# A two-layer Mamba + mixture-of-experts kernel: layer 0's shared output added to X from PSUM, rows for the scatter kept in memory, four gathers ahead, 23 tiles, ScalarE's side pieces three steps later

## The reference, cut to what matters

```python
x = x + L0_xattn(ctx, layernorm(x), ...)   # conv, silu, delta, B, C, a scan over 512 positions with 16 states, * silu(z)
x = x + L0_ffn(layernorm(x), ...)          # below
x = x + L1_xattn(ctx, layernorm(x), ...)
x = x + L1_ffn(layernorm(x), ...)          # 8 experts, 2 for each row, shared expert of 1408 with a sigmoid gate

def L0_ffn(x):                             # 8 experts, 1 for each row
    logits = x @ router_w
    expert_idx, score = argmax(logits), sigmoid(max(logits))
    xs = x * score
    out[e rows] = (silu(xs @ gate_w[e]) * (xs @ up_w[e])) @ down_w[e]
    shared = (silu(x @ shared_gate_w) * (x @ shared_up_w)) @ shared_down_w
    return out + shared
```

## Time and profile before

| | |
|---|---|
| median of 3 runs | 2397.37 us |
| the profiled execution's own time | 2404.08 us |
| its span, first to last instruction | 2402.1 us |
| mean granted TensorE clock | 0.903 |
| busy: PE, DVE, ACT, POOL | 1959.0, 1415.0, 855.9, 989.3 us |
| SP's DMA queue | 326.21 MB, 39.7% of 16 engines |
| GpSimd's DMA queue | 25.17 MB, 3.1% |

### The profile page before, as it was taken

The page is one execution under the profiler, slowest core; times in us unless marked ns, Lnnn a source line. Parts: engine busy times, 40 slices in busy tenths (PEclk is TensorE's granted clock), DMA queues, the critical chain, the costliest instruction groups (busy, mean ns, idle before and its releaser), DMA issues. The chain is left out here.

```text
span 2402.1 us, 18775 instructions
## 1 busy us (share of the span) xinstructions
PE 1959.0 (82%) x5107; PEld 901.3 (38%) x5107; DVE 1415.0 (59%) x1962; ACT 855.9 (36%) x1392; POOL 989.3 (41%) x889
## 2 busy tenths in 40 slices
PE   8837678788787795599999973889599999999990
PEld 2212233233233341144444432445255555555540
DVE  6869988888887878797888844654010111111113
ACT  5545545364544444555656420110011111111110
POOL 0057766666575665887777731211400000000005
PEclk9968889899898997799999985999799999999995
DMA  5044354302203004368687645211654555455536
GB/s 185 22 194 105 140 110 107 112 5 99 89 8 153 1 14 155 138 225 339 224 305 277 215 153 189 68 50 58 242 179 152 180 180 166 160 179 180 175 123 214
DMA packets 100992, 352.50 MB, mean 147 GB/s; under 512 B 15200, under 2 KB 15200, under 8 KB 82464
## 3 DMA queue, kind: packets, MB, share of 16 engines
q1 hardware_dynamic: 93216, 326.21, 39.7%
q0 software_dynamic: 7680, 25.17, 3.1%
HBM read 288.29 MB, written 63.05 MB: 146 GB/s over the span
## 5 line engine op out<-in xcount | busy, mean ns | idle before, releaser
L561 POOL TENSOR_TENSOR work<-work,big 128x512 f32<-128x512 f32 x512 | 658.5, 1291 | 265.7 <-DVE bank L608 263.9
L474 PE MATMUL bank<-work,ident 128*128 128x512 f32 x928 | 536.9, 693 | 226.5 <-DVE work L592 175.9
L608 DVE TENSOR_TENSOR_SCAN bank<-bank,work 128x512 f32<-128x512 f32 x512 | 624.9, 1221 | 137.5 <-ACT bank L528 88.9
L528 ACT ACTIVATE bank<-work,An 128x512 f32<-128x512 f32 x512 | 345.9, 691 | 256.2 <-DVE work L592 253.1
L474 PEld LDWEIGHTS bank<-work,ident 128*128 128x128 f32 x928 | 179.5, 216 | 521.6 <-DVE work L592 333.7
L592 DVE TENSOR_TENSOR work<-bank,big 128x512 f32<-128x512 f32 x512 | 343.9, 672 | 9.1 <-PE bank L474 8.8
L1655 POOL DMA_INDIRECT W<-ys_d,slot x32 | 33.9, 1059 | 644.4 <-PEq L1642 634.9
L1612 PE MATMUL bank<-Y,big 128*128 128x512 f32 x528 | 263.6, 596 | 0.0
L1195 DVE SCALAR_TENSOR_TENSOR work<-work,bank 128x352 f32<-128x352 f32 (+1 forms) x63 | 36.6, 581 | 329.0 <-ACT work L1185 328.9
L957 PE MATMUL bank<-W,work 128*128 128x512 f32 x384 | 198.6, 622 | 0.0
L1173 ACT COPY work<-bank 128x512 f32<-128x512 f32 x63 | 36.9, 585 | 396.9 <-PE bank L1158 396.9
(11 more groups left out here) (249 smaller groups left out, 2252.8 us busy)
## 6 DMA issues: line engine op xcount, KB each, us to landing
big<-bc_d SPq DMA_DIRECT2D x64, 1024.0 KB, 6.7
work<-gate SPq DMA_DIRECT2D x39, 704.0 KB, 4.2
work<-up SPq DMA_DIRECT2D x39, 704.0 KB, 4.1
W<-gate SPq DMA_DIRECT2D x24, 1024.0 KB, 4.9
W<-up SPq DMA_DIRECT2D x24, 1024.0 KB, 5.5
W<-down SPq DMA_DIRECT2D x24, 1024.0 KB, 5.4
work<-down SPq DMA_DIRECT2D x39, 512.0 KB, 3.8
work<-xs_d SPq DMA_DIRECT2D x63, 256.0 KB, 4.4
```

Of the source, the lines that this page charges most:

```text
L474: nc.tensor.matmul(YS[:, :], ident[:, :], hC[ring(g * NS + u[0])], start=v == 0, stop=v == len(units[g]) - 1).then_inc(sum_done, 1)
L528: nc.scalar.activation(H[i % 4][:, :], delta[g % 2], ACT.Exp, scale=An[vb // B][:, g % NJ, i:i + 1]).then_inc(dA_done, 1)
L561: nc.gpsimd.tensor_tensor(dBu[i % 2], du[g % 2], Bb[:, i, :], ALU.mult).then_inc(dBu_done, 1)
L608: nc.vector.tensor_tensor_scan(H[i % 4][:, :], H[i % 4][:, :], dBu[i % 2], 0.0, ALU.mult, ALU.add).then_inc(scan_done, 1)
```

## The change

1. Layer 0's shared output stays in PSUM until VectorE adds it to X (`added`, 16 times, at the places where ScalarE copied it, the last of a batch in the very piece that makes it). `copy_y`, `yo`, `sh_d`, its 16 stores, its 16 loads and the 16 additions L1468 go.
2. X now no longer gives the normalised rows. So SP stores each `xn` to `xn_d` as it is made (16 stores, `xn_out`), SP loads them for the scatter, and ScalarE scales them by the router's weight. VectorE's `norm` and the gate's tanh of ScalarE, which overwrite `xn`, wait for these stores too.
3. In the scan ScalarE does its side pieces LAG = 3 steps after their place (`gate` excepted).
4. Layer 0 has 23 tiles of sorted rows and not 24.
5. Layer 1's feed-forward: four gather buffers and gathers issued four ahead; weights loaded in three widths, gate and up beside each other.
6. Small operations go: a copy of the mean on GpSimd, two on VectorE in the routing.

```diff
-        self.tiles += (self.tiles % 2, 0)[k]
...
-                    side.step("act", act, vb, n)
+                    if vb <= B:
+                        side.gate("act", act, vb, *divmod(n, NS))
+                    if s >= side.LAG:
+                        side.step("act", act, *divmod(s - side.LAG, NJ * NS))
+                for s in range(GROUPS * NS - side.LAG, GROUPS * NS):
+                    side.step("act", act, *divmod(s, NJ * NS))
...
             def gate(self, name, eng, b, j, i):
...
-                        self.past(eng, "xtr_done", b * NJ - NJ + (j + 1 if j else 0))
+                        used = b * NJ - NJ + (j + 1 if j else 0)
+                        self.past(eng, "xtr_done", used)
+                        self.past(eng, "xn_out", used * 16)
                     nc.scalar.activation(self.zth, v, ACT.Tanh).then_inc(self.S["zt_done"], 1)
...
+                    done = {(2, 3): 0, (3, 3): 1, (NJ, 1): NJ - 2, (NJ, 7): NJ - 1}.get((r, m))
+                    if done is not None:
+                        past(dve, "d_done", t0 + done + 1)
+                        nc.vector.tensor_tensor(X[:, t0 + done, :], X[:, t0 + done, :], self.TB[:, :], ALU.add).then_inc(S["added"], 1)
...
             def norm(self, dve, b, t0, r):
                 self.past(dve, "rstd_done", t0 + r + 1)
                 self.past(dve, "xtr_done", t0 + r)
+                self.past(dve, "xn_out", (t0 + r) * 16)
...
-                        act.wait_ge(S["y_out"], (t0 + max(r - 1, 0)) * 16 + 1)
                         nc.scalar.activation(self.sg, self.G[:, :], ACT.Tanh, scale=0.5).then_inc(S["s_done"], 1)
...
             def sync(self, sp, b, t0, n, at):
-                for r, m in at:
-                    for tile in ([r - 2] if m == 5 and 2 <= r else []) + ([NJ - 1] if r == NJ and m == 7 else []):
-                        self.past(sp, "yo_done", t0 + tile + 1)
-                        sp.dma_start(sh_d[t0 + tile], self.yo).then_inc(self.S["y_out"], 16)
+                for tile in ([0] if n == self.START - 1 else []) + [r + 1 for r, m in at if m == 6 and r < NJ - 1]:
+                    self.past(sp, "xn_done", t0 + tile + 1)
+                    sp.dma_start(xn_d[t0 + tile], self.xn).then_inc(self.S["xn_out"], 16)
...
             def scatter(self, name, eng, t):
-                if name == "act" and 0 <= t < T:
+                if name == "sp" and 0 <= t < T:
...
+                    eng.dma_start(self.rows[t % 8], xn_d[t]).then_inc(self.row_in[t % 8], 16)
+                if name == "act" and 0 <= t - 1 < T:
+                    t -= 1
...
+                    eng.wait_ge(self.row_in[t % 8], t // 8 * 16 + 16)
+                    nc.scalar.activation(self.rows[t % 8], self.rows[t % 8], ACT.Copy,
+                                         scale=wgt[:, 0, t:t + 1]).then_inc(self.row_done, 1)
...
+            WIDE = ((0, 2), (2, 6), (6, NF))
...
-                    for t in range(NJ):
-                        load(t)
...
+                    for c, (lo, hi) in enumerate(WIDE):
+                        for o in (0, FS):
+                            sp.dma_start(sgu[:, :, o + lo * P:o + hi * P], src[:, :, o + lo * P:o + hi * P]).then_inc(w_in[c], 16)
...
                     def gather(t):
-                        at_least(pool, C["x_done"], t - 1)
+                        at_least(pool, C["x_done"], t - 3)
...
-                            if p == r:
-                                dve.wait_ge(sh_in[t % 2], (t // 2 + 1) * 16)
-                                V.tensor_tensor(X_t, X_t, sh_b[t % 2], ALU.add).then_inc(C["sum_done"], 1)
```

More of the change, by code:

```diff
@@ L177, in program @@
         bc_d = dram("bc_d", [2 * B, 32, L])
-        sh_d = dram("sh_d", [T, P, D])
         xn_d = dram("xn_d", [T, P, D])
@@ L853, in step @@
                 last = isinstance(b, int) and b == B
-                if not last or n < NS:
+                if name != "act":
                     self.gate(name, eng, b, *divmod(n, NS))
@@ L863, in gate @@
             def gate(self, name, eng, b, j, i):
-                first = isinstance(b, int) and b == 0
-                if first and j == 0:
+                first = b == 0
+                if first and j == 0 or b == B and j:
                     return
@@ L1027, in scalar @@
                 for r, m in at:
-                    if m == 3 and 2 <= r < NJ:
-                        copy_y(r - 2)
                     if (m == 5 if r < NJ else m == 2) and r:
@@ L1218, in __init__ @@
                 self.row_done, self.out_done = sem("t0_row_done"), [sem(f"t0_scattered{q}") for q in range(8)]
+                self.row_in = [sem(f"t0_row_in{q}") for q in range(8)]
                 self.routed, self.cleared = sem("t0_routed"), sem("t0_rows_cleared")
@@ L1276, in step @@
                         eng.wait_ge(self.routed, 1)
-                        self.past(eng, "y_out", 16 * T)
+                        self.past(eng, "added", T)
+                        self.past(eng, "xn_out", 16 * T)
                     self.ex.before(name, eng)
@@ L1318, in stage_ffn1 @@
             v, zth = [wk(8 + j) for j in range(NJ)], [wk(12 + j) for j in range(NJ)]
-            sh_b, ys_b = [wk(16), wk(17)], [wk(18), wk(19)]
+            ys_b = [wk(16 + q) for q in range(4)]
             rows = [wk(14 + i) for i in range(6)]
@@ L1362, in _ @@
                 def _(sp):
-                    def load(t):
-                        at_least(sp, C["sum_done"], t - 1)
-                        sp.dma_start(sh_b[t % 2], sh_d[t]).then_inc(sh_in[t % 2], 16)
                     def keep(t):
```

80 lines of the change are left out of this document (29 added, 51 removed).

## The result

The kernel after takes **2450.41 us** (median of 4 runs, 2447.88 to 2454.62) beside 2398.09 of the kernel before (4 runs): ratio 1.0222, 95% interval 1.0200 to 1.0243. It is slower by 52 us; the forecast was 2383, range 2350 to 2410.

The account below looks back on a forecast made before the run. In scan batches 1 to 3 VectorE and TensorE stop each other; TensorE bounds batch 6 and the stretch from 1712 us. Terms summing to -14.2 took the profiled 2404.1 to 2389.9, or 2383.2 from the median; range 2350 to 2410.

Parts of the forecast that it names:

- store behind zeros(1), with the clock: Batch 1: tile 1's xn store lands behind the 9984 KB zeros on SP's queue; +51 us, plus 1.5 for TensorE's clock.
- no sh_d, batches 1 to 3: Scan batches 1 to 3: shared output added from PSUM ends waits for ScalarE's tanh and dA; -7 us each, -21.
- batch 4: Scan batch 4, frames packed in 36 steps, dA stalls following TensorE's lateness; -3 us, ends -8 and +3.
- scatter, batch 5: Batch 5: rows scaled by ScalarE after dA slow GpSimd's alternation of scatter and dBu; +5 us, ends 0 and +12.
- 23 tiles: End of scan: TensorE loses 16 passes and the last down product with its weight load; -17 us, ends 12 and 19.
- start and fronts of the feed-forward: Layer 1's feed-forward: -15.7 us at its start without the sh_d wait, -12 in the fronts of the other batches.
- ScalarE's pieces later: Batches 5 to 7: the later pieces remove part of VectorE's 40.9 us of waits for dA; -3 us, ends 0 and -9.
- Rival B: Scan: ScalarE's lateness costs what it saves, 1.4 us in each of 23 expert tiles; 2410 us, 18 in 100.
- Rival C: Scan: VectorE's waits for dA go wholly, half of 102.5 us of waits for ScalarE recovered; 2358 us, 15 in 100.
- term of -15.7: Start of layer 1's feed-forward: the 19.24 us sh_d wait goes, the fourth gather is late next; ends -11 and -20.
- The later fronts: Feed-forward's other three batches: each front loses four additions and 1 to 2 us of waits; -12 us, ends -8 and -14.4.
- The sign named for B: Scan: L1195 or TensorE waiting for ScalarE in every tile, and batches 6 and 7 over 155 us.

Follow-up runs that it names:

- LAG 0: Changed kernel with ScalarE's side pieces at their own step: 2373.91 us; with both zero stores also moved to step 10 of batch 0: 2320.79 us.
- zeros early: Changed kernel with both 9984 KB zero stores issued at step 10 of batch 0, ahead of any xn store: 2398.81 us.
- LAG 3 then 0: Changed kernel with both zero stores at step 10 of batch 0, ScalarE's side pieces three steps late only up to batch 4: 2367.02 us.
- LAG 1: Changed kernel with both zero stores at step 10 of batch 0 and ScalarE's side pieces one step late: 2313.14 us.

## Why the prediction was wrong, by its own steps

| step | forecast | measured | by |
|---|---|---|---|
| store behind zeros(1), with the clock | +52.5 | +51.6 (LAG 3), +53.1 (LAG 0) | zeros early |
| no sh_d, batches 1 to 3 | -21 | -20.2 | 486.5 to 466.3, 23 tiles alone against LAG 0 |
| batch 4 | -3 | -8.1 | 174.4 to 166.3, the same two |
| scatter, batch 5 | +5 | +2.0 | 162.8 to 164.8, the same two |
| 23 tiles | -17 | -17.3 | alone |
| start and fronts of the feed-forward | -27.7 | -34.3 | 923.5 to 889.2, the same two |
| **ScalarE's pieces later** | **-3** | **+76.5** | LAG 0 against LAG 3 |

All rows but the first and the last are read at LAG 0. The other terms were forecast at -11 in sum and came to -26 (the pause in it, +52.5 for 51.6 to 53.1), so they hid some 15 us of the miss of 79.5 in the last row; by the medians 67 was left. One step failed, *ScalarE's pieces later*: -3 us, with ends of 0 and -9, so with no end above nothing. It was costed by what it could take away (the 40.9 us for dA) and not by what it makes late. It does take those waits away, 40.9 to 2.5 us, and puts larger ones in their place.

Rival B had the mechanism and nearly its size, 1.4 us in each expert tile for 1.27 measured. It failed in its condition and in its price. The condition was that VectorE has 2.3 us to spare a tile in batch 6, from (151.9 - 130.8) / 9.1. That spare time is a mean; it lies in waits of other steps (for dA and dBu), and a wait put in front of the scan moves what comes after it. Added up for batches 5 to 7, VectorE's waits were 74.6 us before and 111.6 after, 37 us more; the three batches grew by 35.6. The price of B left out two things: the preparation of delta, which stands in the same list of ScalarE and turns 1.3 us into 4 to 8 in eight tiles (47 us of the 63.7), and batches 1 to 4, which pay 46 us by the run with LAG 3 then 0. Of these B had the larger part in words alone, that TensorE waits for the later copies; it gave it no price. The shared tiles' tanh had 1.4 us once a batch, in the term of batches 1 to 3; two tiles a batch wait for it, 2.1 and 4.9 us. Rival C's condition came true, the waits for dA went, and brought nothing, as the new waits were larger.

The scatter in batch 5 was forecast for ScalarE three steps late; its +2.0 was measured without the lag, and what it costs by itself with it no run shows. With it, GpSimd waited 4.27 and 4.83 us for two row scalings, which stood behind steps of the preparation on ScalarE. The longer one:

```profile
1021.13 1.28 ACT L512 ACT_TABLE_LOAD   x1
...
1024.80 0.71 ACT L1247 ACTIVATE Y<-Y,wgt 128x512 f32<-128x512 f32 x1
...
1025.78 1.01 POOL L1255 DMA_INDIRECT xs_d<-Y,slot  x1 [4.83 <-ACT Y L1247]
```

At the feed-forward's start the term of -15.7 measured -21.9 (TensorE's wait 47.8 to 25.9), beyond its end of -20: I had taken 3.6 us from one gather to the next from the earlier trace rows. Four queued gathers came quicker: they landed at 1521.27, 1523.21, 1524.30 and 1525.46, so 1.9, 1.1 and 1.2 us apart. The rule of the Trainium skill that a DMA engine takes the queue rows in turn ("DMA: Bandwidth & Descriptors", "Queues, rings and completion order"), which I weighed and did not follow, had given an estimate of 1.5 us a gather. That lies near these distances, but they don't test the rule: GpSimd issues the gathers 1.3 us apart (1515.07 to 1518.90) and each takes 6.2 to 6.8 us to land, so the distance of the landings can be that of the issues. Its gain was also added up wrong: three distances, each 2.1 us shorter, are 6.3 us and not 9, and 6.2 is what was measured beyond my term. In the kernel before gathers 0 and 1 were issued 1.3 us apart too and landed 3.6 apart (6.06 and 8.33 us after their issues), why stays open; gathers 2 and 3 were issued only when a buffer came free (1441.91 and 1445.50) and landed 6.9 and 7.1 us later. So a distance of two landings was no measure of what a gather needs. The later fronts measured -9.3 (14.4 to 5.1 us) for -12.

Of what was to be seen, right were the pause and its place, no 7 us wait of the shared product by `sh_d`, VectorE's wait for the down product at the batch ends, the scan's short tail, and the start of the feed-forward (its first transposes 22 us after the start, for 28 forecast). Wrong were batch 1 near 207 (215.3) and batches 2 and 3 near 156 (162.2 and 166.9). The sign named for B, the experts' product waiting in nearly every tile with batches 6 and 7 over 155 us, is just what came (165.5 and 158.2).

## What to carry to other kernels

A reordering on one engine's list is to be costed by whom each moved instruction serves, the copies for TensorE as well as the tanh for VectorE, and by how far that engine can run ahead at all: here the ring gave three steps; a lag of one won 8 us on the changed kernel, a lag of three lost 78. Spare time of an engine as a mean over a stretch was no cover for a wait at a fixed place in its loop. A wait for a small store was as long as the 9984 KB transfer ahead of it on its queue: move the large one to where nobody waits, or the small one to another queue. Two remedies for the same wait didn't add: together (LAG 1) batches 1 to 4 took 637.0 us, alone 632.6 and 628.0.

## What the runs showed of the hardware beyond that

SP's own issue of the 256 KB store behind the zeros took 32.02 us (row of 328.28 above) where the `sh_d` store, issued when the same zeros had 6.2 us to go, took 0.34. With LAG 0 it took 32.00. So a small transfer right behind a large one can hold up the issuing engine too, and with it what stands behind on its list; which limit it meets there, no run shows. On ScalarE's queue the same store was issued in 0.35 us and landed 10.3 us later beside the zeros, a mean of 25 GB/s; the zeros took 53.1 us for 52.5.
